# The 128 scatters of a slot table, moved behind the first four score pieces of an attention layer with routed experts

## The chip, the cores and the metric

The kernel runs on one core of one Trainium2 chip. The metric is the device time of one execution in microseconds (us); shorter is better. Of a set of runs the median is given. The profile is of one execution of its own, with every instruction recorded.

## What is computed

One transformer layer on `x` of 4 sequences of 1024 tokens with 256 features: a layer norm, causal attention with 16 heads of 16 features, and on the same normalised rows a mixture of 16 experts (four per token) beside a shared one. All three are summed.

```python
xn = _layernorm(x)
# attention
q, k, v = (split_heads(xn @ W + b) for W, b in ((Wq, bq), (Wk, bk), (Wv, bv)))
scores = where(causal, einsum('bhqd,bhkd->bhqk', q, k) / sqrt(16), -inf)
attn_out = merge_heads(softmax(scores) @ v) @ Wo + bo
# experts
topk_w, topk_idx = top_k(softmax(xn @ gate_w.T), 4)       # weights divided by their sum
combine = zeros(T, 16).at[arange(T)[:, None], topk_idx].add(topk_w)
a = silu(einsum('th,ehi->tei', xn, w_gate)) * einsum('th,ehi->tei', xn, w_up)
y = einsum('tei,eih->th', a * combine[:, :, None], w_down)
y = y + (silu(xn @ sw_gate) * (xn @ sw_up)) @ sw_down
out = x + attn_out + y
```

## The kernel before

The program has three parts, one behind the other, each a block with one hand-written instruction stream per engine. Engines wait for each other by semaphores (`wait_ge(sem, n)`, `then_inc(sem, 1)`).

`prepare` normalises the rows, makes queries, keys, values and the logits of the router, and keeps the expert weights in two half-precision parts. `route` picks four experts for each of the 4096 tokens and gives each of the 16384 token-expert pairs a place in a table of 144 tiles of 128 slots, sorted by expert. At its end SBUF holds `entry` (token number and weight of each pair) and `slot_i` (its place). The table itself, `slot_d`, lies in DRAM and has been filled with a padding row.

`attention_and_experts` has 16 attention groups (four heads of one sequence each). A group has 20 slots; each slot is one score piece: PE writes scores to `stp` (L1125, `st_done`), ACT takes their exponential (`exps`, L1484, `exp_done`), and PE multiplies these `probs` with the values (L1144). Before that a group needs its row maxima: 18 pieces, which PE makes (L1100, L1083) and DVE reduces (`reduce_piece`, L1314); DVE closes them and makes `nm` (L1326), which SP copies into the queries' rows (L993). The maxima of group 0 stand alone at the head of the block, those of each later group are spread over the slots of the one before. Between the slots a planner has spread the expert work in a fixed order: units of a gate-and-up product (`gate_up`, L1221), an activation, a turn (L1233) and a down product (L1248). First come 48 units of the shared expert for 24 tiles, then the 144 routed tiles, then the last shared units. A routed tile needs its token rows, which PE turns (`turn_rows`, L1191, waits for `xg_in`).

All indirect transfers are on the queue of POOL (GpSimd), in this order: 128 scatters of `entry` into `slot_d` (L931, semaphore `scattered`), the wait for all of them, the load of the finished table into `slots` (L934, `sl_in`), eight gathers of token rows into `XG` (L942, one buffer each), the wait for the stores of the 24 shared tiles (`out_st`), and then by turns a scatter-add of a finished tile (L949) and a gather ten tiles ahead. Attention results go out by L958.

Of the kernel before, what the change touches and what calls it, by code (L numbers as in the profile page):

```python
# [756 lines left out]
def attention_and_experts(nc, s):  # L757
# [5 lines left out]
    with ExitStack() as ctx:  # L763
# [58 lines left out]
        STEPS = [(q, t, max(0, t * P - q * CH)) for q in range(QC) for t in range((q + 1) * CH // P)]  # L822
        NST = len(STEPS)
        DIAG = [st for st, (q, t, _) in enumerate(STEPS) if t * P >= q * CH]
        SCP = []
        for st, (_, _, q0) in enumerate(STEPS):
            SCP += [(st, (0, 1))] if CH - q0 <= CH // 2 else [(st, (0,)), (st, (1,))]
# [65 lines left out]
        def adds_before(r):  # L893

            return r // 2 + (0 if r % 2 else 1 + sum(1 for k in HALF_AFTER if k < r))

        def adds_before_half(b, h):
            k = half_after(b, h)
            return 1 + k // 2 + 1 + sum(1 for x in HALF_AFTER if x < k)
# [20 lines left out]
        @block.gpsimd  # L920
        def _(pool):
            pool.memset(part[:, :, 1], -3.0e38).then_inc(a_const, 1)
            pool.memset(YA[:, 0], 0.0).then_inc(a_const, 1)
            pool.memset(sel[:, :], 0.0).then_inc(a_const, 1)
            pool.wait_ge(a_const, 3)
            pool.affine_select(out=sel[:, :], in_=sel[:, :], compare_op=ALU.not_equal, fill=1.0, base=-DK,
                               pattern=[[-32, 4], [0, 32]], channel_multiplier=1).then_inc(sel_made, 1)
            pool.dma_start(s.out[T:T + P, :], YA[:, 0]).then_inc(added[0], 16)

            for i in range(TT * TOPK):  # L930
                pool.indirect_dma_start(s.slot_d, bass.IndirectOffsetOnAxis(ap=s.slot_i[:, i:i + 1], axis=0),  # L931
                                        s.entry[:, i, :], None).then_inc(scattered, 16)
            pool.wait_ge(scattered, 16 * TT * TOPK)
            pool.dma_start(slots[:, :, :].rearrange("p u a -> p (u a)"),  # L934
                           s.slot_d.rearrange("(p u) a -> p (u a)", p=P)).then_inc(sl_in, 16)
            pool.wait_ge(sl_in, 16)

            def gather(r):
                q = r % GB
                if r >= GB:  # L940
                    pool.wait_ge(xp_done, r - GB + 1)
                pool.indirect_dma_start(XG[:, q].rearrange("p a c t -> p (a c t)"), None, s.xrow_d,  # L942
                                        bass.IndirectOffsetOnAxis(ap=slots[:, r, 0:1], axis=0)).then_inc(xg_in[q], 16)

            def scatter_add(r):
                pool.wait_ge(yo_done, ST + r + 1)
                if adds_before(r):
                    pool.wait_ge(added[r % 2], 16 * adds_before(r))
                pool.indirect_dma_start((s.out, s.acc_d)[r % 2], bass.IndirectOffsetOnAxis(ap=slots[:, r, 0:1], axis=0),  # L949
                                        Y[:, r % YB], None, compute_op=ALU.add).then_inc(added[r % 2], 16)  # L950

            def add_attention(b, h, adds):

                t0 = h * KT // 2
                pool.wait_ge(ya_done, b * KT + t0 + KT // 2)
                pool.wait_ge(added[0], 16 * adds)
                row = (b * KT + t0) * P
                pool.dma_start(s.out[row:row + CH, :].rearrange("(t p) d -> p t d", p=P),  # L958
                               YA[:, t0:t0 + KT // 2], accum_op=ALU.add).then_inc(added[0], 16)

            for r in range(GB):
                gather(r)
            for i in range(YB):
                pool.wait_ge(out_st[i], 16 * ST // YB)
            pool.wait_ge(cleared, 32)
            for r in range(UT):
                if r == 0:
                    for x in range(GB, AHEAD):
                        gather(x)
                scatter_add(r)  # L970
                if r + AHEAD < UT:
                    gather(r + AHEAD)
                if r in HALF_AFTER:
                    b, h = HALF_AFTER[r]
                    add_attention(b, h, adds_before_half(b, h))
            for c in range(2):
                pool.wait_ge(added[c], 16 * ALL_ADDS[c])
            for b in range(B):
                pool.dma_start(s.out[b * N:(b + 1) * N, :], s.acc_d[b * N:(b + 1) * N, :],
                               accum_op=ALU.add, max_dma_last_dim=8192).then_inc(merged, 16)  # L980
            pool.wait_ge(merged, 16 * B)
            for h in range(2):
                add_attention(B - 1, h, ALL_ADDS[0])
            pool.wait_ge(added[0], 16 * (ALL_ADDS[0] + 2))
# [572 lines left out]
```

## Time and profile before

| | us |
|---|---|
| median of three runs | 1186.36 |
| the three runs | 1182.34 to 1187.22 |
| span of the profiled execution | 1354.9 |
| PE busy in it | 1007.9 (74%) |
| DVE busy | 866.0 (64%) |
| ACT busy | 654.5 (48%) |
| POOL busy | 579.2 (43%) |

The profiled execution is another one than the timed runs, and its span is 168.5 us longer than their median. Engines: PE is TensorE, with its weight loads on a row of their own (PEld), DVE VectorE, ACT ScalarE, POOL GpSimd, SP SyncE. L931 is line 931 of the kernel. In the rows of a timeline the columns are start, duration, engine, line, operation, written tile and read tiles, shapes, count, and in brackets the idle time of the engine before it and what ended that; "remote" there is a releaser that the trace does not show, and "issue" time in which the engine waited for nothing that it shows.

### The profile page before, as it was taken

The page shows a single profiled execution, that of the slowest core. Times are in us where ns is not written, and L with a number is a line of the kernel's source. Part 1 is how long each engine was busy: PE and PEld are TensorE (multiplying, and loading weights), DVE is VectorE, ACT ScalarE, POOL GpSimd, SP SyncE. Part 2 cuts the span into 40 slices and gives each one's busy share as a digit, 9 for nine tenths or more (in the row PEclk, how much of TensorE's full clock was granted, in tenths as well). Part 3 has the DMA queues.
Part 4 walks back from the last instruction along what each step waited for, and adds up shares of the span by engine and source line. Part 5 has one row for each costly group of instructions (what it writes and reads, how often), then busy time and mean ns, then how long its engine had stood idle before and what let it go on. Part 6 is the DMA issues. An engine that isn't in the chain of part 4 may idle for free.

```text
span 1354.9 us, 26394 instructions
## 1 busy us (share of the span) xinstructions
PE 1007.9 (74%) x8634; PEld 525.7 (39%) x8634; DVE 866.0 (64%) x1784; ACT 654.5 (48%) x1219; POOL 579.2 (43%) x531
## 2 busy tenths in 40 slices
PE   2788121010399999898998989998988989899885
PEld 1555010000144444444544444454444445444433
DVE  6888831000288887777777676676767676677553
ACT  3778100000154545565566666556666665566341
POOL 6333177776200000454366666435656553464100
PEclk9888555555599999899999999999989999899888
DMA  6899450010113131443545355354535353444702
GB/s 175 270 297 283 125 180 1 1 34 1 43 56 105 54 104 48 88 85 75 89 80 112 63 111 95 66 89 78 111 57 112 56 112 64 88 71 73 134 17 31
DMA packets 99484, 126.41 MB, mean 93 GB/s; under 512 B 24873, under 2 KB 83514, under 8 KB 98834
## 3 DMA queue, kind: packets, MB, share of 16 engines
q0 software_dynamic: 41632, 60.79, 25.0%
q1 hardware_dynamic: 57730, 63.99, 16.1%
q8 instruction: 77, 1.26, 0.4%
q14 instruction: 45, 0.37, 0.1%
HBM read 71.63 MB, written 57.80 MB: 96 GB/s over the span
## 4 chain that ended last, share of the span: by engine, by line
PE 53%; DVE 10%; another core or an unknown queue 10%; issue 9%; ACT 2%; SPq 1%; DMA 1%; POOL 0%; ACTq 0%; DVEq 0%
PE gup L1221 12%; PE pvp L1144 10%; PE outs L1248 9%; DVE part L1314 6%; PE smp L1100 6%; PE turn L1233 4%; PE stp L1125 4%; PE outs L1151 3%; PE turn L1191 3%; PE smp L1083 1%; ACT probs L1484 1%; DVE hf L1371 1%; DVE sg L1366 1%; DMA Qs<-nm 1%
## 5 line engine op out<-in xcount | busy, mean ns | idle before, releaser
L1484 ACT ACTIVATE probs<-stp 128x1024 f32<-128x1024 f32 (+1 forms) x320 | 300.4, 939 | 424.4 <-remote 205.2
L1314 DVE TENSOR_REDUCE part<-smp 128x2 f32<-128x256 f32 (+2 forms) x372 | 345.9, 951 | 140.0 <-remote 72.5
L942 POOL DMA_INDIRECT XG<-xrow_d,slots x144 | 146.8, 1019 | 247.0 <-DMA out<-Y 201.7
L1221 PE MATMUL gup<-gu_w,XC 128*128 (+1 forms) x1152 | 212.8, 321 | 32.7 <-issue 21.8
L1100 PE MATMUL smp<-Ks,Qs 48*128 48x128 f16 (+2 forms) x744 | 112.5, 341 | 103.7 <-DVE part L1314 52.4
L1248 PE MATMUL outs<-dn_w,h 88*128 (+1 forms) x1248 | 183.6, 280 | 0.1
L949 POOL DMA_INDIRECT out<-Y,slots x72 | 117.1, 1626 | 139.1 <-ACT Y L1517 107.8
L1144 PE MATMUL pvp<-probs,Vs 128*32 128x512 f32 (+3 forms) x1536 | 168.8, 512 | 0.8 <-DVE probs L1413 0.7
L949 POOL DMA_INDIRECT acc_d<-Y,slots x72 | 114.7, 1594 | 123.7 <-ACT Y L1517 104.6
L1221 PEld LDWEIGHTS gup<-gu_w,XC 128*128 128x128 f16 x1152 | 107.2, 99 | 96.1 <-issue 43.5
L931 POOL DMA_INDIRECT slot_d<-entry,slot_i x128 | 124.3, 971 | 41.6 <-issue 41.6
L1366 DVE SCALAR_TENSOR_TENSOR sg<-th,gup 128x176 f32<-128x176 f32 x208 | 69.8, 336 | 106.6 <-ACT th L1490 69.3
L1376 DVE TENSOR_TENSOR h<-turn,h 88x256 f16<-88x256 f32 x208 | 86.6, 416 | 78.1 <-ACT h L1496 67.2
L1248 PEld LDWEIGHTS outs<-dn_w,h 88*128 88x128 f16 x1248 | 123.3, 99 | 29.3 <-issue 2.5
L1496 ACT ACTIVATE h<-turn 88x256 f16<-88x256 f32 x208 | 78.3, 377 | 115.5 <-PE turn L1233 110.5
L1125 PE MATMUL stp<-Qs,Ks 50*128 50x512 f16 (+3 forms) x768 | 118.7, 332 | 16.2 <-DMA Qs<-nm 8.0
L1100 PEld LDWEIGHTS smp<-Ks,Qs 48*128 48x128 f16 x744 | 28.9, 94 | 199.8 <-DVE part L1314 99.8
L1233 PE MATMUL turn<-ident,hf 128*88 128x128 f32 x416 | 87.7, 294 | 22.9 <-issue 17.8
L1413 DVE TENSOR_TENSOR probs<-probs,keepk 128x512 f32<-128x512 f32 x128 | 87.7, 685 | 22.9 <-ACT probs L1484 16.3
L1490 ACT ACTIVATE th<-gup 128x176 f32<-128x176 f32 x208 | 66.4, 319 | 53.8 <-PE gup L1221 35.2
L1501 ACT ACTIVATE XC<-turn 128x512 f16<-128x512 f16 x144 | 85.3, 593 | 5.3 <-PE turn L1191 4.0
L1517 ACT ACTIVATE Y<-outs,slots 128x256 f32<-128x256 f32 x144 | 68.0, 472 | 31.9 <-PE outs L1248 27.9
(170 smaller groups left out, 1109.6 us busy)
## 6 DMA issues: line engine op xcount, KB each, us to landing
rb<-rsum_d SPq DMA_DIRECT2D x60, 128.0 KB
Ks<-k_d SPq DMA_DIRECT2D x96, 64.0 KB
Qs<-q_d SPq DMA_DIRECT2D x96, 64.0 KB
v_d<-V SPq DMA_DIRECT2D x8, 544.0 KB, 4.6
Vs<-v_d SPq DMA_DIRECT2D x16, 272.0 KB, 3.0
acc_d<-YA SPq DMA_DIRECT2D x1, 4224.0 KB
X<-L_attn_x POOLq DMA_DIRECT2D x8, 512.0 KB, 5.0
xrow_d<-XR SPq DMA_DIRECT2D x8, 512.0 KB, 5.0
```

The lines of the kernel that those rows point to most:

```text
L931: pool.indirect_dma_start(s.slot_d, bass.IndirectOffsetOnAxis(ap=s.slot_i[:, i:i + 1], axis=0), s.entry[:, i, :], None).then_inc(scattered ...
L942: pool.indirect_dma_start(XG[:, q].rearrange("p a c t -> p (a c t)"), None, s.xrow_d, bass.IndirectOffsetOnAxis(ap=slots[:, r, 0:1], axis= ...
L949: pool.indirect_dma_start((s.out, s.acc_d)[r % 2], bass.IndirectOffsetOnAxis(ap=slots[:, r, 0:1], axis=0), Y[:, r % YB], None, compute_op= ...
L1100: last = pe.matmul(banks[:, e, col:col + w], Qs[rows, buf, j, t * P:(t + 1) * P], Ks[rows, buf, j, k0:k0 + w], start=i == 0, stop=k0 + w < ...
L1125: last = pe.matmul(stp[:, e, i * w:(i + 1) * w], Ks[rows, buf, j, t * P:(t + 1) * P], Qs[rows, buf, j, q * CH + q0:(q + 1) * CH], start=i ...
L1144: last = pe.matmul(pvp[32 * h:32 * h + 32, q0:CH], Vs[:, buf, o:o + 2 * DK], probs[:, st % PB, h * w:(h + 1) * w], start=t == 0, stop=t == ...
L1221: last = pe.matmul(gup[:, 0:2 * I], columns[:, a, h], weights_of(s.gu_w, e, b, h, slice(0, 2 * I)), start=n == 0, stop=n == 5)
L1233: last = pe.transpose(hp[:, c * P:(c + 1) * P], hf[:, v % FB, c * IP:(c + 1) * IP], s.ident[:, :])
L1248: last = pe.matmul(yp, h16[:, v % 2, a, c], weights_of(s.dn_w, e, b, c, slice(0, D)), start=begin and n == 0, stop=end and n == 5)
L1314: last = dve.tensor_reduce(part[:, g % 2, k0 // CH, :, j, t], banks[:, :, col:col + w], AX.X, ALU.max)
L1413: dve.tensor_tensor(block, block, s.keepk[:, :].rearrange("p (h k) -> p h k", h=1).broadcast_to([P, 4, P]), ALU.min).then_inc(masked, 1)
L1484: act.activation(to, of, ACT.Exp, scale=float(DK) ** -0.5 / QS ** 2).then_inc(exp_done, 1)
```

## The change

On POOL, ahead of the loop of the 128 scatters, a wait is added: they begin only when ACT has finished the exponentials of four score pieces, which are the first four of attention group 0.

```diff
             pool.dma_start(s.out[T:T + P, :], YA[:, 0]).then_inc(added[0], 16)
 
+            pool.wait_ge(exp_done, 4)
             for i in range(TT * TOPK):
                 pool.indirect_dma_start(s.slot_d, bass.IndirectOffsetOnAxis(ap=s.slot_i[:, i:i + 1], axis=0),
                                         s.entry[:, i, :], None).then_inc(scattered, 16)
```

## Rows read from the trace of the kernel before

**Rows 1.** The page: busy tenths and granted clock in 40 slices of 33.9 us

```profile
PE 2788121010399999898998989998988989899885
POOL 6333177776200000454366666435656553464100
PEclk9888555555599999899999999999989999899888
```

**Rows 2.** Stretches: length; busy PE, PEld, DVE, ACT, POOL (count); clock, DMA, GB/s

```profile
171.00:370.70 199.70, 26.57 (x172) 10.41 (x173) 29.56 (x41) 5.16 (x9) 132.55 (x137) 0.51 0.15 42
370.70:526.40 155.70, 144.91 (x1271) 71.94 (x1269) 128.17 (x254) 77.82 (x140) 0.00 (x0) 0.99 0.26 75
526.40:1354.90 828.50, 739.66 (x6395) 384.16 (x6395) 570.35 (x1037) 475.73 (x876) 385.43 (x292) 0.96 0.44 81
```

**Rows 3.** Timeline of 165 to 372 us, single rows

```profile
170.96 1.07 POOL L931 DMA_INDIRECT slot_d<-entry,slot_i  x1 [0.31 <-issue]
172.39 1.22 DVE L1314 TENSOR_REDUCE part<-smp 128x2 f32<-128x1024 f32 x1
...
178.05 1.21 DVE L1314 TENSOR_REDUCE part<-stp 128x2 f32<-128x1024 f32 x1
...
182.51 0.53 PE L1083 MATMUL smp<-maskq,idh 64*128 64x128 bf16 x8
...
197.15 1.29 DVE L1314 TENSOR_REDUCE part<-smp 128x2 f32<-128x512 f32 x2 [10.06 <-remote]
...
317.75 0.97 POOL L931 DMA_INDIRECT slot_d<-entry,slot_i  x1 [2.97 <-issue]
...
325.29 0.61 PE L1125 MATMUL stp<-Qs,Ks 50*128 50x512 f16 x2 [4.41 <-issue]
...
362.06 1.02 ACT L1484 ACTIVATE probs<-stp 128x1024 f32<-128x1024 f32 x1 [20.73 <-remote]
```

**Rows 4.** Waits from 165 to 365 us: total, times, longest

```profile
ACT probs L1484 <- remote: 200.3, 2, 179.6
DVE part L1314 <- remote: 122.5, 9, 32.6
```

**Rows 5.** Timeline: last maximum piece and first score piece of group 0

```profile
281.90 1.29 DVE L1314 TENSOR_REDUCE part<-stp 128x2 f32<-128x256 f32 x2 [32.37 <-remote]
...
291.14 0.61 PE L1125 MATMUL stp<-Qs,Ks 50*128 50x512 f16 x2 [3.96 <-DMA Qs<-nm]
```

**Rows 6.** Timeline: the fourth exponential, and PE's first two turns of gathered rows

```profile
369.86 0.81 ACT L1484 ACTIVATE probs<-stp 128x768 f32<-128x768 f32 x1 [0.77 <-PE stp L1125]
...
526.45 0.38 PE L1191 MATMUL turn<-ident,XG 128*128 128x128 f16 x4 [0.44 <-DVE h L1376]
...
534.26 0.63 PE L1191 MATMUL turn<-ident,XG 128*128 128x128 f16 x4
```

**Rows 7.** Timeline of POOL: last scatter, slot table, first gather, ninth gather

```profile
335.59 0.97 POOL L931 DMA_INDIRECT slot_d<-entry,slot_i  x1 [0.30 <-issue]
337.98 0.60 POOL L934 DMA_DIRECT2D slots<-slot_d  x1 [1.42 <-DMA slot_d<-entry,slot_i]
340.56 1.01 POOL L942 DMA_INDIRECT XG<-xrow_d,slots  x1 [1.97 <-DMA slots<-slot_d]
...
552.14 0.95 POOL L942 DMA_INDIRECT XG<-xrow_d,slots  x1 [201.74 <-DMA out<-Y]
```

**Rows 8.** Line 942 (gathers), 335 to 360 and from 526: ns min/median/max, first, last

```profile
L942 POOL DMA_INDIRECT XG<-xrow_d,slots x8: 953/957/1010, 340.6 to 349.4; - x8
L942 POOL DMA_INDIRECT XG<-xrow_d,slots x136: 955/1010/1431, 552.1 to 1217.5; - x136
```

**Rows 9.** Stretches behind the hole, columns as in rows 2

```profile
362.00:366.00 4.00, 2.51 (x13) 1.13 (x14) 3.94 (x7) 2.31 (x4) 0.00 (x0) 0.50 0.11 33
366.00:369.00 3.00, 3.00 (x17) 0.89 (x16) 0.68 (x2) 0.61 (x2) 0.00 (x0) 0.65 0.00 0
```

**Rows 10.** Groups of instructions from 370 to 1355 us: DVE's reductions

```profile
L1314 DVE TENSOR_REDUCE part<-smp 128x2 f32<-128x1024 f32 (+1 forms) x355 | 330.9, 953 | 50.9 <-PE smp L1083 29.8 <-PE smp L1100 17.1 <-remote 1.9
```

## The prediction

> **What bounds the kernel now.** I read the page first. The row of slices [rows 1] shows three stages: a preparation in which all engines and the DMA work, a hole in which only POOL is busy (PE at 0 to 2 tenths, granted clock half), and a long stage in which PE stands at 8 or 9 tenths. The table of stretches [rows 2] puts numbers to them: up to 171.0 us preparation and routing; from 171.0 to 370.7 the hole, 199.7 us with 26.6 us of PE work in it; from there to the end 984.2 us in which PE is busy 884.6 us (144.91 + 739.66), its clock 0.96 to 0.99. The last stage is bound by PE, and its instructions stand in a fixed order, so a wait of PE there is added to the end.
>
> The hole is the stretch of the 128 scatters. The timeline [rows 3] shows what happens in it: a scatter takes 0.97 us and the next follows after 0.30 (the last one stands in [rows 7]), while the first eight row-maximum pieces run undisturbed, one in 1.13 us (the third begins at 172.39, the eighth at 178.05). Later DVE and ACT stand still although PE's work on which they wait had ended: the piece that PE worked on at 182.51 (0.53 us long) is reduced only at 197.15, and the score piece of 325.29 gets its exponential at 362.06. The table of waits [rows 4] adds this up: DVE 122.5 us and ACT 200.3 us (overlapping) on a releaser that the trace does not show. Only signals that go out from PE are late; PE itself answers DVE at once.
>
> **Profile against the timed runs.** The span is 1354.9 us, the median of the three runs 1186.4. How long would the hole be without those waits? Eighteen pieces at 1.13 us are 20 us; from the last reduction to the first score piece 8 us (283.19 to 291.14) [rows 5], score piece and first exponential 2 us (0.61 and 1.02 and the way between them) [rows 3]; exponentials 2 to 4 end 8.6 us after the second began (362.06 to 370.67) [rows 3, 6]. That is 38 us, where the profile has 199.7. So 161.7 us of waits stand in the profiled execution, and 1354.9 - 161.7 = 1193 us without them. That is within 7 us of the median, before anything around the span, for which I have no row and which I carry at nothing. So the timed runs hardly have those waits. An upper bound: if all 99.6 us of PE's idle time after 370.7 were missing in the timed runs, 1186 - 171 - 38 - 885 = 92 us of waits could still be in them; the estimate nearest to the rows is none. I therefore work on a timeline of 171 + 38 + 984 us, and every length below is taken from stretches without those waits.
>
> **The change part by part.** One wait is added on POOL; nothing is removed, and no engine but POOL gets an instruction. Behind the wait stand, in POOL's order: the 128 scatters, the wait for all of them, the load of the slot table, eight gathers, the wait for the shared tiles' stores, and all further gathers and scatter-adds. Ahead of it stand the constants, the `sel` matrix and the zero store, so nothing that the first four exponentials need is held, and there is no circle. Two engines wait for what is queued behind: PE for the first gathered tile (`turn_rows(0)`), ACT for the slot table, which it needs later than PE its tile. SP issues nothing for the scatters and is not moved.
>
> Before, the scatters begin with the hole at 171.0 and the first tile is there some 172 us later, that is 134 us after the fourth exponential on the timeline without waits (172 - 38). After, they begin with the fourth exponential. So the question is whether the chain on POOL fits between that exponential and the first use of a tile.
>
> The cover: the fourth exponential ends at 369.86 + 0.81 = 370.67, PE's first row turn begins at 526.45 [rows 6], which is 155.8 us. In it PE is busy 144.91 of 155.7 us at clock 0.99 [rows 2], so it cannot be much shorter or longer in the timed runs. Before the change, 155.8 - 134 = 22 us are to spare.
>
> The chain: 0.3 us to the first scatter; the scatters from 170.96 to 335.59 + 0.97 = 336.56, 165.6 us [rows 3, 7], less one pause of 2.97 where 0.30 is usual [rows 3] = 162.9; from there to the first gather's issue 4.0 us (drain, slot table there and back, 340.56) [rows 7]; the gather 0.96 us, and for its landing, which has no row, the 2.0 us that the slot table took behind its issue (338.58 to 340.56). Sum 170.2, so PE gets the tile 14.4 us late. That is with DVE idle: in the hole DVE is busy 29.56 of 199.7 us, in the new place 128.17 of 155.7 [rows 2]. The nearest rows of POOL beside a busy DVE are the gathers: median 0.957 us in the hole, 1.010 in the last stage [rows 8]. If scatters gain the same 0.053 us, 128 of them take 6.8 us more and the tile is 21.2 us late. The ends are 14.4 and 21.2. A gather moves whole rows, a scatter two words, so part of that growth need not apply: I take the middle, 17.8 us.
>
> The other gathers follow 1.3 us apart, while PE wants the second tile 7.8 us after the first (534.26) [rows 6]: one wait, not eight. POOL then waits for the shared tiles' stores anyway (552.14 in the trace, 201.7 us of idle time) [rows 7]; that point moves with PE, so nothing adds up behind it.
>
> The clock: PE idles for these 18 us. When it resumed after the hole, the granted clock was 0.50 of full (1.2 of 2.4 GHz) from 362 to 366, 0.65 in the mean to 369, and it is 0.99 over the next stretch [rows 2, 9]; 2.51 + 3.00 us of PE work at mostly half speed cost about 2.8 us. I add 2.8; a shorter idle time may cost nothing, so its bounds are 0 and 2.8.
>
> The gain: the pieces of the first group lose their companion on POOL. The first eight ran at 1.13 us beside it, so on the timeline without waits the gain is nothing; its bound is the 92 us above, if the timed runs have such waits after all. Sum: 1186.4 + 17.8 + 2.8 = **1207 us**.
>
> **A rule that speaks against the change.** The Trainium skill, page SBUF — State Buffer, section SBUF: two separate sides, says that a DMA issued from GpSimd has its descriptors written by that engine, which is locked out while VectorE holds the port pair that they share; its example is about 620 ns alone against 3100 beside a copy. By these figures 128 scatters would take an estimated 128 x 2.5 = 317 us more and the sum would be 1524 at worst, where no DVE operation lets them through. The trace agrees in direction only: 0.957 against 1.010 us [rows 8].
>
> **The rivals.**
> Signals late in the timed runs too (faster). If part of the hole's 161.7 us is in the timed runs, moving the scatters behind the first group's maxima takes it away. For it: [rows 4]; and in the last stage, with POOL issuing the same kind of operation at a lower density, DVE's such waits are 1.9 us in all [rows 10]. Against it: the sum of 1193 us leaves no room. At half of the bound, 46 us, the time would be 1186 - 46 + 20.6 = 1161; it shows as faster from 27 us of waits on. 0.15.
>
> The chain fits (no change). If a scatter without the recorder takes 1.15 us from start to start instead of 1.275, the chain is 16 us shorter (128 x 0.125) and PE waits hardly at all: 1186 to 1190. For it: 0.30 us of each are dispatch, of which recording may be a part. Against: nothing else of the profile looks 10% too long, since 1193 is 0.6% from the median. 0.22.
>
> Scatters starved by DVE (clearly slower), the skill's rule above: with the largest gather, 1.431 us [rows 8], for all, 128 x 0.46 = 59 us more than beside an idle DVE, 14.4 + 59 + 2.8 behind the median: 1263. It decides as soon as scatters take over 1.1 us on average. One row speaks for it, the median against it. 0.04.
>
> The late signals come with the scatters into the loaded stretch (slower): if the timed runs have them beside any dense stream of scatters, PE's partners there stop as in the hole, at most the same 92 us on top; half of it gives 1253. The before runs already overlap 124 us of scatters with attention and show none. 0.04.
>
> That the wait does nothing can be left out: the fourth exponential can't be done when POOL arrives.
>
> **How the numbers follow.** Forecast 0.55, with 1192 to 1216 as its own range (from 14.4 us with no cost of the clock, less 8 us if POOL's pace is 5% quicker, up to 21.2 + 2.8 + the pause of 2.7 and the rest for rounding). No change 0.22, faster 0.15, the two dear cases 0.08. About 0.5%, 6 us, is what a measurement of this kernel can tell from no change. Faster 0.15, same 0.22, slower 0.63. The range 1161 to 1216 holds the forecast, the case of no change and the half of the gains that is up to 26 us net; it leaves out the larger gains and the dear cases, 0.16 in all.
>
> **What would show it.** In the profile after: scatters that begin just behind the fourth exponential; 128 of them in 163 to 171 us; the first gather at some 167 to 175 us behind that exponential; a wait of PE for a gathered tile before the first row turn of 14 to 24 us, followed by a few us at half clock; an unchanged last stage. The maxima of the first group should take about 20 us instead of 113, so the profiled span may fall by far more than the timed runs move. The prediction is wrong if PE has no wait at the first turn, if scatters run at less than 1.2 us or more than 1.4 from start to start, or if the median falls with the span.

## The result, and the profile after

| | before | after |
|---|---|---|
| median of the timed runs, us | 1184.35 | 1207.26 |
| runs, us | 1182.22 to 1187.22 | 1202.61 to 1211.81 |
| ratio (95% interval) | | 1.0206 (1.0166 to 1.0246) |
| span of the profiled execution, us | 1354.9 | 1210.2 |

The change makes the kernel 2.1% slower, 22.9 us between the medians; 1207 was forecast. The profiled span fell by 145 us all the same. Whoever had compared the two profiles alone would have read a gain of 11%.

The page of after, busy tenths in 40 slices of 30.3 us each:

```profile
span 1210.2 us, 26394 instructions
...
PE   2877436999982999999999989898989898999875
POOL 6433200777766266346656553565666624544000
PEclk9888756999996999999999999999999999999888
```

The hole of [rows 1] is gone. What is left of it is one slice in which PE stands at 2 tenths and its clock at 6, the thirteenth. The table of stretches (length; busy time of PE, PEld, DVE, ACT and POOL with counts; granted clock, DMA share, GB/s) answers to [rows 2]:

```profile
171.00:208.40 37.40, 24.11 (x177) 10.07 (x173) 29.26 (x41) 5.34 (x9) 0.20 (x1) 0.58 0.60 194
208.40:385.80 177.40, 144.90 (x1271) 71.96 (x1269) 129.53 (x255) 78.36 (x140) 131.27 (x132) 0.94 0.26 70
385.80:1210.20 824.40, 740.76 (x6395) 385.02 (x6395) 568.43 (x1035) 476.02 (x875) 391.89 (x298) 0.96 0.44 82
```

The first group's maxima with its first four exponentials take 37.4 us where [rows 2] has 199.7. The second stretch holds the same work as before, 144.9 us of PE, and is 177.4 us long in place of 155.7. The timeline of its two ends and of POOL in between shows what was added (start, duration, engine, line, operation, tiles, idle time before and its releaser; lines have moved by one):

```profile
207.53 0.81 ACT L1485 ACTIVATE probs<-stp 128x768 f32<-128x768 f32 x1 [0.77 <-PE stp L1126]
208.64 1.49 POOL L932 DMA_INDIRECT slot_d<-entry,slot_i  x1 [37.44 <-ACT probs L1485]
...
360.07 0.96 POOL L932 DMA_INDIRECT slot_d<-entry,slot_i  x1 [3.40 <-issue]
...
377.90 0.97 POOL L932 DMA_INDIRECT slot_d<-entry,slot_i  x1 [0.30 <-issue]
380.30 0.60 POOL L935 DMA_DIRECT2D slots<-slot_d  x1 [1.43 <-DMA slot_d<-entry,slot_i]
383.00 1.01 POOL L943 DMA_INDIRECT XG<-xrow_d,slots  x1 [2.09 <-DMA slots<-slot_d]
385.82 0.61 PE L1192 MATMUL turn<-ident,XG 128*128 128x128 f16 x4 [21.54 <-DMA XG<-xrow_d,slots]
```

The scatters follow the fourth exponential at once, the table goes to DRAM and back, the first gather is issued, and PE, whose next instruction in its fixed order needs that tile, has waited 21.54 us for it. ACT and DVE wait behind PE. The rest takes 824.4 us against 828.5 [rows 2]. That stretch is not the same in every execution: from PE's first row turn to the end the thirteen profiles of this case have 814.6 to 828.5 us. The longest is the first profile of before, and the five kernels in which PE waits for a tile have 815.6 to 826.8. So a few us more or less in this stretch say nothing on the change.

### The profile page after: what moved, and what is told of

The parts are those of the page before. It is cut to its first block, busy times and chain, and to the rows that moved or that the text cites. A ratio compares the mean times of both kernels' runs of the same rounds, so it can differ in the third digit from the quotient of the medians.

```text
span 1210.2 us, 26394 instructions
## 1 busy us (share of the span) xinstructions
PE 1006.8 (83%) x8634; PEld 526.9 (44%) x8634; DVE 864.2 (71%) x1784; ACT 655.7 (54%) x1219; POOL 584.3 (48%) x531
## 4 chain that ended last, share of the span: by engine, by line
PE 52%; POOL 11%; issue 9%; DVE 9%; DMA 2%; ACT 2%; SPq 1%; ACTq 0%; DVEq 0%
POOL slot_d L932 11%; PE gup L1222 10%; PE pvp L1145 10%; PE outs L1249 8%; DVE part L1315 6%; PE smp L1101 6%; PE turn L1234 4%; PE stp L1126 4%; PE outs L1152 4%; PE turn L1192 3%; PE smp L1084 1%; DMA Qs<-nm 1%; ACT probs L1485 1%; DVE sg L1367 1%; DVE probs L1414 1%
## 5 line engine op out<-in xcount | busy, mean ns | idle before, releaser
L1315 DVE TENSOR_REDUCE part<-smp 128x2 f32<-128x256 f32 (+2 forms) x372 | 346.0, 951 | 52.2 <-PE smp L1084 33.2
L943 POOL DMA_INDIRECT XG<-xrow_d,slots x144 | 147.8, 1026 | 65.0 <-issue 40.8
L932 POOL DMA_INDIRECT slot_d<-entry,slot_i x128 | 128.5, 1004 | 79.2 <-issue 41.8
L1101 PE MATMUL smp<-Ks,Qs 48*128 48x128 f16 (+2 forms) x744 | 113.0, 342 | 37.2 <-DVE part L1315 20.7
L1234 PE MATMUL turn<-ident,hf 128*88 128x128 f32 x416 | 87.3, 292 | 21.1 <-issue 17.8
L1414 DVE TENSOR_TENSOR probs<-probs,keepk 128x512 f32<-128x512 f32 x128 | 87.7, 685 | 21.1 <-ACT probs L1485 20.1
L1502 ACT ACTIVATE XC<-turn 128x512 f16<-128x512 f16 x144 | 85.4, 593 | 27.4 <-PE turn L1192 27.4
L1192 PE MATMUL turn<-ident,XG 128*128 128x128 f16 x576 | 57.7, 224 | 36.2 <-DMA XG<-xrow_d,slots 21.5
```

The lines of the kernel that those rows point to most:

```text
L1101: last = pe.matmul(banks[:, e, col:col + w], Qs[rows, buf, j, t * P:(t + 1) * P], Ks[rows, buf, j, k0:k0 + w], start=i == 0, stop=k0 + w < ...
L1234: last = pe.transpose(hp[:, c * P:(c + 1) * P], hf[:, v % FB, c * IP:(c + 1) * IP], s.ident[:, :])
L1315: last = dve.tensor_reduce(part[:, g % 2, k0 // CH, :, j, t], banks[:, :, col:col + w], AX.X, ALU.max)
L1414: dve.tensor_tensor(block, block, s.keepk[:, :].rearrange("p (h k) -> p h k", h=1).broadcast_to([P, 4, P]), ALU.min).then_inc(masked, 1)
```

## The experiments

Two theories stood against each other. By the theory of the late chain, the only thing that costs is that POOL's chain of scatters, table and gather ends after PE wants the first tile: a delay is free up to a slack and costs one for one beyond it. By the rivals, each us of delay costs something, or the company of the scatters in the loaded stretch costs. A third question was where the hole of the first profile comes from.

**The kernel before, once more.** No edit.

> The kernel before, unchanged, for a second profile and for the noise of the comparison. Theory A (the stretch of 161.7 us in which PE's signals are late belongs to that one profiled execution): the hole is gone or has another length, the span is near the median, 1183 to 1195 us, the scatters begin near 171 and the first gathered tile is there 14 to 24 us ahead of PE's first row turn. Theory B (profiling this kernel always brings the hole, the timed runs have none): a span of about 1355 again, with a ratio of 1.00 between the timed runs.

Ratio 1.0003 (0.9978 to 1.0028), span 1181.7 us. The hole is not there: the table of waits has no unknown releaser between 165 and 365 us, where [rows 4] has 122.5 and 200.3 us. The page, the stretches, POOL's first and last steps and PE's first turn of this execution:

```profile
PE   2877526999999998999999989998989899999875
```

```profile
171.00:208.50 37.50, 24.14 (x175) 10.02 (x172) 29.07 (x41) 5.31 (x9) 28.35 (x31) 0.57 0.65 194
208.50:364.30 155.80, 145.02 (x1272) 72.11 (x1270) 128.18 (x254) 77.86 (x141) 107.62 (x108) 0.99 0.30 84
364.30:1181.70 817.40, 734.10 (x6395) 383.14 (x6395) 569.23 (x1037) 475.43 (x876) 386.19 (x292) 0.97 0.44 82
```

```profile
171.44 1.06 POOL L931 DMA_INDIRECT slot_d<-entry,slot_i  x1 [0.31 <-issue]
...
346.27 1.01 POOL L942 DMA_INDIRECT XG<-xrow_d,slots  x1 [2.12 <-DMA slots<-slot_d]
...
364.35 0.38 PE L1191 MATMUL turn<-ident,XG 128*128 128x128 f16 x4 [0.44 <-DVE h L1376]
```

The landing of its gathers, from their issue:

```profile
DMA to landing us min/median/max: 2.9/2.9/2.9
```

This is the profile against which the change has to be read. The first stage has the length that the prediction had worked out (37.5 us; 38), the cover too (155.8; 155.8). A gather is in SBUF 2.9 us after its issue here, so the first tile is there at 349.1 and PE wants it at 364.3: **15.2 us of slack**. With the scatters 37.2 us later (208.64 against 171.44), PE should wait 37.2 - 15.2 = 22.0; it waited 21.5.

**Three other delays.** The semaphore of the added wait was varied (the note behind the #, which is no part of the kernels, says which kernel has which):

```diff
-            pool.wait_ge(exp_done, 4)
+            pool.wait_ge(smax_done, 9)     # start_max9; exp_done, 1 in start_exp1; exp_done, 12 in start_exp12
```

> The scatters wait for the ninth row-maximum piece of group 0 in place of the fourth exponential, so they begin some 9 us later than before instead of 37. Theory A (the cost is the lateness of the first gathered tile, behind about 15.7 us of slack = 37.2 us of delay less the 21.5 us that PE waits in the profile after): the delay lies within the slack, PE does not wait for the tile, 1184 us, no change within 0.4%. Rival (each us of delay costs, 22.9 us / 37.2 = 0.62 per us): 1184 + 5.5 = 1190 us.

> The scatters wait for the first exponential only, which ends at 198.8 in the profile after, 27.4 us behind the start of before. Theory A: PE waits 27.4 - 15.7 = 11.7 us for the first tile, with some 2 us at half clock behind it: 1184 + 13.7 = 1198 us. Rival (a cost for each us of delay): 1184 + 17 = 1201. Rival (the cost comes from the scatters' company in the loaded stretch, which begins with this exponential): the whole 23 us, 1207.

> The scatters wait for the twelfth exponential, which ends at 231.9 in the profile after, 60.6 us behind the start of before. Theory A: PE waits 60.6 - 15.7 = 45 us for the first tile and works some 2 us' worth at half clock: 1184 + 47 = 1231 us. Rival (a cost for each us of delay): 1184 + 37 = 1221. Rival (company in the loaded stretch): no more than after the change, 1207, since the scatters have no more company than there.

The delay is the start of the first scatter less 171.44. These rows have the first scatter and PE's first row turn of the three kernels, in the order above:

```profile
178.80 1.06 POOL L932 DMA_INDIRECT slot_d<-entry,slot_i  x1 [8.78 <-PE smp L1084]
...
363.61 0.38 PE L1192 MATMUL turn<-ident,XG 128*128 128x128 f16 x4 [0.44 <-DVE h L1377]
```

```profile
198.86 1.07 POOL L932 DMA_INDIRECT slot_d<-entry,slot_i  x1 [28.23 <-ACT probs L1485]
...
374.92 0.61 PE L1192 MATMUL turn<-ident,XG 128*128 128x128 f16 x4 [11.56 <-DMA XG<-xrow_d,slots]
```

```profile
231.91 1.06 POOL L932 DMA_INDIRECT slot_d<-entry,slot_i  x1 [61.27 <-ACT probs L1485]
...
406.75 0.61 PE L1192 MATMUL turn<-ident,XG 128*128 128x128 f16 x4 [44.84 <-DMA XG<-xrow_d,slots]
```

| scatters behind | delay, us | delay - 15.2 | PE's wait, us | ratio (95%) | cost by the ratio, us |
|---|---|---|---|---|---|
| nothing | 0 | - | 0 | 1.0003 (0.9978 to 1.0028) | 0 |
| the ninth maximum piece | 7.4 | - | 0 | 0.9975 (0.9951 to 1.0000) | -3 |
| the first exponential | 27.4 | 12.2 | 11.6 | 1.0113 (1.0078 to 1.0148) | 13 |
| the fourth (the change) | 37.2 | 22.0 | 21.5 | 1.0206 (1.0166 to 1.0246) | 24 |
| the twelfth | 60.5 | 45.3 | 44.8 | 1.0357 (1.0301 to 1.0414) | 42 |

(The cost is the ratio less 1, times 1180.8 us, the median of the kernel before in these comparisons, or its own 1184.35 for the change.) PE's wait follows the delay one for one beyond the slack, to within 0.7 us. A cost for each us of delay, at the 0.62 us that the change shows, would have given 4.6 us at the ninth piece, 17 at 27.4 and 37 at 60.5. The last two lie within the intervals of their ratios (9 to 17.5 us, and 35.5 to 49); it is the ninth piece that rules this rival out, with at most 0 us by its interval (2.7 us when timed again, below) and PE without a wait. Company alone would have given the same 23 us in the last three rows; it falls, since 23 lies above the first of those intervals and below the second.

The ninth piece looked like a small gain. The same kernel timed once more:

> The scatters behind the ninth maximum piece once more with more rounds; its first ratio was 0.9975 with an interval that ended at 1.000. By the theory of slack the ratio is 1.000, within 0.998 to 1.002. If giving the first maxima nine undisturbed us is a gain, it stays at 0.996 to 0.998 (4 us).

The ratio was 0.9995 (0.9968 to 1.0023), here with a delay of 8.2 us. The seven to eight undisturbed us of the first maxima give nothing that can be measured.

**The change, without PE's dependence on it.** Eight gathers go ahead of the wait, with row numbers that are there from the start:

```diff
+            for r in range(GB):
+                pool.indirect_dma_start(XG[:, r]..., None, s.xrow_d,
+                                        bass.IndirectOffsetOnAxis(ap=s.entry[:, 4 * r, 0:1], axis=0)).then_inc(xg_in[r], 16)
             pool.wait_ge(exp_done, 4)
...
-            for r in range(GB):
-                gather(r)
```

> As after the change, but the first eight gathers are issued ahead of the wait and take their row numbers from a list that is there from the start (tokens in order), not from the table; so the first eight tiles hold other rows than they should. The scatters lie where the change puts them. Theory A (the cost is PE's wait for the first gathered tile): that wait is gone; the table is then wanted by the first weighted output some 21 us later, just when it lands: 1184 to 1189 us, no change against the kernel before. Rival (the scatters' company in the loaded stretch costs): 1205 to 1207, as after the change.

PE's wait is gone; its first turn stands at 363.23:

```profile
363.23 0.38 PE L1193 MATMUL turn<-ident,XG 128*128 128x128 f16 x4 [0.44 <-DVE h L1378]
```

The ratio is 1.0045 (1.0014 to 1.0076): 19 of the 24 us are gone with the wait, 5 us are left. To see whose they are, the same kernel again, and one with the early gathers but the scatters from the start:

> The first eight gathers ahead of the wait, from the list of tokens, once more with more rounds (the first eight tiles hold other rows than they should). Its first ratio was 1.0045. If its 5 us are real, the ratio stays between 1.002 and 1.007; if they were noise, it comes to 0.998 to 1.002. Either way PE shows no wait for a gathered tile at its first row turn.

> The same eight early gathers from the list of tokens (again other rows in the first eight tiles), but with the scatters from the start, as before the change. If the 5 us come from the early gathers or from the other rows, the ratio is that of the run with the wait, 1.002 to 1.007. If they come from the scatters' place (their company in the loaded stretch, or a table that lands just when it is wanted), it is 0.998 to 1.002 here and higher there.

1.0048 (1.0026 to 1.0071) with the wait and 1.0033 (1.0000 to 1.0065) without it. So the 5 us are real. The second ratio, some 4 us, makes it likely that most of them come with the early gathers or the other rows in the first eight tiles, which these runs don't separate; but its interval begins at nothing, so this is not shown. The two ratios differ by 0.0015, 1.8 us, less than the width of either interval: whether the scatters' place has a part in the 5 us stays open.

**Half the scatters in the new place.**

```diff
-            for i in range(TT * TOPK):
+            pool.wait_ge(exp_done, 4)
+            for i in range(TT * TOPK // 2):
...
```

The wait for the scatters is halved with them.

> As after the change, with 64 scatters in place of 128, so half of the tokens never get to an expert and their slots hold the padding row. Theory A: the chain on POOL is 64 x 1.3 = 83 us shorter, the first tile is there some 60 us ahead of PE's turn, no wait: 1184 us. Rival (company in the loaded stretch, per scatter): half of the cost stays, 1184 + 11 = 1195 us.

```profile
298.99 1.01 POOL L943 DMA_INDIRECT XG<-xrow_d,slots  x1 [2.41 <-DMA slots<-slot_d]
...
365.36 0.38 PE L1192 MATMUL turn<-ident,XG 128*128 128x128 f16 x4 [0.43 <-DVE h L1377]
```

Ratio 0.9992 (0.9963 to 1.0020), no wait of PE: the first gather is issued at 298.99, the first turn begins at 365.36. Sixty-four scatters beside the loaded stretch cost nothing that can be measured (2.4 us at most by the interval), and neither does the wait on POOL by itself.

**The scatters in the old place, the table late.**

```diff
-            pool.dma_start(slots...).then_inc(sl_in, 16)
-            pool.wait_ge(sl_in, 16)
+            for n in range(15):
+                pool.dma_start(slots...).then_inc(sl_in, 16)
+                pool.wait_ge(sl_in, 16 * (n + 1))
...
```

ACT's own wait for the table, further down, counts all fifteen loads too.

> As before the change (scatters from the start), but behind the scatters the finished table is loaded 15 times, each load waited for, some 14 x 2.6 = 36 us in place of the 37 us of delay ahead of the scatters. Theory A (only the end of the chain counts): PE waits some 20 us for the first tile and the time is that of the changed kernel, 1204 to 1209 us. Rival (it is the place of the scatters that costs): 1184 us.

Ratio 1.0230 (1.0203 to 1.0257). The first gather is issued at 387.07, 40.8 us later than in the second profile of before; less the slack, 25.6, and PE waited 25.4:

```profile
387.07 1.01 POOL L943 DMA_INDIRECT XG<-xrow_d,slots  x1 [2.15 <-DMA slots<-slot_d]
...
389.81 0.61 PE L1192 MATMUL turn<-ident,XG 128*128 128x128 f16 x4 [25.38 <-DMA XG<-xrow_d,slots]
```

The scatters lie as before, and the cost is that of the change: the end of the chain makes it, not the place of the scatters.

**The change once more**, beside these three:

> The changed kernel once more, beside its relatives on one chip: 1207 us, a ratio of 1.02 and 21 us of wait at PE's first row turn by both theories; its profile shows whether PE's signals are ever late in it.

Ratio 1.0229 (1.0187 to 1.0271), 22.52 us of wait, span 1212.3, and again no wait for an unknown releaser:

```profile
385.55 0.61 PE L1192 MATMUL turn<-ident,XG 128*128 128x128 f16 x4 [22.52 <-DMA XG<-xrow_d,slots]
```

## Why the prediction was right, point by point

The mechanism is the one that was forecast. The scatters take 170.2 us from 208.64 on, the first gather is issued 174.7 us behind the fourth exponential, PE waits 21.5 us for one tile and then works at half clock for a few us. The sizes of some terms were off.

**The hole was the profile's own.** The step that decided the sign was to take 161.7 us of waits out of the profile before anything was costed, because 1193 us came within 7 us of the median and 1355 did not. The second profile of before, at 1181.7 us, shows it right. The rival that let part of the hole into the timed runs had no ground, and its 92 us of room were not there. The rival by which scatters are quicker in the timed runs fell too: the medians lost 22.9 us, about what the trace shows (21.5 of wait and 1.9 of clock, below).

**The cover** was 155.8 us by [rows 6] and is 155.8 in the second profile of before. In the profile after, PE's last work ahead of the wait ends at 364.28 (385.82 - 21.54), 155.9 us behind the fourth exponential (208.34).

**The chain was a little undersized**: 170.2 us beside an idle DVE, 177.0 beside a busy one, the middle taken, 173.6. From 208.34 to 385.82 it was 177.5. Two terms were too small. First the scatters' own time: 1.004 us on average after, against 0.971 in the hole (124.3 us for 128 on the page of before; [rows 7] show one). The page's groups (line, engine, operation, tiles, count; busy us, mean ns; idle us and releaser) of after and of the second profile of before:

```profile
L932 POOL DMA_INDIRECT slot_d<-entry,slot_i x128 | 128.5, 1004 | 79.2 <-issue 41.8
```

```profile
L931 POOL DMA_INDIRECT slot_d<-entry,slot_i x128 | 127.6, 997 | 43.0 <-issue 43.0
```

That is 0.033 us each, 4.2 us for 128, where the middle had 3.4 and the upper end 6.8. The size was near by luck, since the way was another: the prediction took 0.053 us from the gathers and let it apply to each scatter, but in after 117 of the 128 take no more than 1.00 us, as beside an idle DVE, and the other eleven, 1.13 to 1.68 us long, make up the whole 4.2 us.

Second the pause of [rows 3], 2.97 us, which the prediction took out as an accident (2.7 us). It stands behind the 113th scatter in all twelve traces of kernels with 128, the first profile of before among them: 2.97 there, 4.25 in the second, 3.40 after the change, 2.96 to 4.84 in all. It is part of the chain. So the lateness was 21.5 us and not 17.8; the stated ends were 14.4 and 21.2, and the pause had been left out of both.

**The clock** was put at 2.8 us. After the wait the granted clock is at half (1.2 of 2.4 GHz) first, as [rows 9] had shown behind the hole:

```profile
364.30:385.80 21.50, 0.00 (x0) 0.00 (x0) 1.73 (x3) 0.81 (x1) 14.02 (x16) 0.55 0.10 26
385.80:389.00 3.20, 3.18 (x18) 1.34 (x18) 0.40 (x2) 0.92 (x2) 2.59 (x3) 0.50 0.43 124
389.00:392.00 3.00, 2.94 (x30) 1.26 (x22) 1.47 (x3) 1.03 (x2) 2.09 (x4) 0.75 0.32 92
```

The second row turns after the change and in the second profile of before:

```profile
394.78 0.39 PE L1192 MATMUL turn<-ident,XG 128*128 128x128 f16 x4
```

```profile
371.39 0.63 PE L1191 MATMUL turn<-ident,XG 128*128 128x128 f16 x4
```

From PE's first to its second row turn it is 8.96 us (385.82 to 394.78) against 7.04 in the second profile of before (364.35 to 371.39): 1.9 us. In the four other profiles with a wait, of 11.6 to 44.8 us, it is 8.9 to 9.7, in the six other profiles without one and without the hole 6.8 to 7.9; it does not grow with the wait. So the sum by the traces is 21.5 + 1.9 = 23.4, where the prediction had 17.8 + 2.8 = 20.6 and the medians differ by 22.9. That the forecast of 1207 met the time more closely than its terms is luck: it started from the first median of before, 1186.4, 2 us above the later one.

**The slack of before** was put at 22 us and is 15.2. The prediction had taken the length of before's chain from the hole, where scatters have no company. Of the 6.6 us between, 3.3 are the scatters' own time (127.6 against 124.3 us) and 1.3 the longer pause. The number did not enter the sum, since the chain behind the exponential was worked out by itself; for start_exp1 it would have about halved the forecast cost.

**VectorE beside the scatters.** The dear case, in which DVE starves the scatters, did not come: their mean rose from 0.971 to 1.004 us, and the longest of after took 1.68. The traces also tell which of DVE's operations stand behind the long ones. Each of the eleven overlaps one of two multiplications whose inputs both lie in SBUF, the mask on the exponentials (L1414) or the scaling of a group's output (L1350). Ten of the twelve scatters that begin while such a multiplication runs are long; of seventeen that are under way when it begins, one is. The row reductions (L1315), which overlap far more scatters, leave them at 0.96 to 1.00 us where no such multiplication joins them:

```profile
254.58 0.69 DVE L1414 TENSOR_TENSOR probs<-probs,keepk 128x512 f32<-128x512 f32 x1 [0.35 <-ACT probs L1485]
254.64 1.48 POOL L932 DMA_INDIRECT slot_d<-entry,slot_i  x1 [0.30 <-issue]
...
260.49 1.28 DVE L1315 TENSOR_REDUCE part<-smp 128x2 f32<-128x512 f32 x2
261.52 1.68 POOL L932 DMA_INDIRECT slot_d<-entry,slot_i  x1 [0.30 <-issue]
261.68 0.68 DVE L1414 TENSOR_TENSOR probs<-probs,keepk 128x512 f32<-128x512 f32 x1
```

In the twelve traces without the hole it is the same for all 115 scatters of more than 1.1 us. No run moves these multiplications, so this is read from the traces and not tested. The Trainium skill, page SBUF — State Buffer, section SBUF: two separate sides, which the prediction cites, gives the shared ports to VectorE for a whole operation only in some cases: in a 2-port mode, or with two SBUF inputs against a GpSimd operation that reads SBUF. The trace agrees with the second case. The estimate of 317 us, a worst case, charged the lock to every scatter; in after it is 4.2 us.

**What stays open** is what made PE's signals late in the first profile. Twelve other profiled executions of this kernel and its variants, three of them with the scatters from the start as before (before once more, early_rows_first and late_table), have no such hole (spans from 1179.5 to 1222.3 us). So it does not come with every profile, nor with every execution that scatters from the start; more can't be said.

## What to carry to other kernels

Put the span of a profile beside the median of the timed runs before reading what bounds it: a wait that is in the profile and has no room in the median is not worth a change. Moving a chain later is free only up to the slack at its last consumer, so work out that end (issue of the last step, landing, first use) rather than what the chain runs beside; beyond the slack PE, which works in a fixed order, passed each us on to the end here. A second profile of the unchanged kernel is the cheapest test of a surprising stretch.

## What the runs showed of the hardware that was not expected

In one execution, while POOL issued 128 scatters one behind the other, signals from PE to DVE, ACT and SP came up to tens of us late (DVE's longest wait of that kind was 32.6 us), and in eleven others with the same 128 scatters they did not. POOL's stream of scatters stops for 3.0 to 4.8 us behind the 113th, wherever in time that falls, also where eight gathers stand ahead of them; a stream of 64 has no such pause. The trace does not say what POOL does in it. A scatter takes POOL up to 0.7 us more than the usual 0.97 when it overlaps a DVE multiplication with both inputs in SBUF, above all when it begins while that runs; beside DVE's row reductions alone it takes no more than 1.00.
